# Crossed 64x64 and 32-row tiles for a convolution kernel's MLP, and fp32 band products from whole-sample row sums without rounded parts

## The reference, cut to what matters

```python
x = x + conv3x3_mixed(_gn(x))      # L0: weights mixed from 3 experts by a softmax of pooled features
x = x + depthwise3x3(abs(_gn(x)))  # L1
x = x + box17x17(_gn(x))           # L2: mean over 17x17, zero padding
x = x + mlp(neighbour_sum(_gn(x))) # L3
```

```python
xn = jnp.repeat(nbr, 8, axis=1)
h = elu(w1 @ xn); h = elu(w2 @ h); h = elu(w3 @ h); h = elu(w4 @ h)
F_int = w5 @ h                     # then mean over groups of four, times 0.1
```

## Time and profile before

| what | value |
| --- | --- |
| median of 3 runs | 909.75 us (906.79 to 911.74) |
| profiled execution, its own time | 903.43 us |
| its span | 901.6 us |
| mean granted TensorE clock | 0.92 of full speed |
| DMA moved | 64.70 MB, mean 72 GB/s |

### The profile page before, as it was taken

The page is one execution under the profiler, slowest core; times in us unless marked ns, Lnnn a source line. Parts: engine busy times, 40 slices in busy tenths (PEclk is TensorE's granted clock), DMA queues, the critical chain, the costliest instruction groups (busy, mean ns, idle before and its releaser), DMA issues.

```text
span 901.6 us, 11198 instructions
## 1 busy us (share of the span) xinstructions
PE 706.5 (78%) x3313; PEld 317.0 (35%) x3313; DVE 676.7 (75%) x1166; ACT 593.4 (66%) x1105; POOL 267.2 (30%) x310
## 2 busy tenths in 40 slices
PE   1424556848897989888888889798989888989993
PEld 0211223224342435343434434353525343434330
DVE  1442744848879887988888878978797789858994
ACT  0120121639777888679876978688977788888883
POOL 2010236212721163223622181116311632271110
PEclk9976678869999999999999999899999999989997
DMA  6528491435512360215320541136022302002201
GB/s 112 119 68 164 83 194 41 88 58 111 113 30 53 78 148 18 64 44 122 74 64 3 120 100 44 37 82 141 19 65 65 65 19 64 19 17 46 54 19 47
DMA packets 54421, 64.70 MB, mean 72 GB/s; under 512 B 6626, under 2 KB 39922, under 8 KB 54386
## 3 DMA queue, kind: packets, MB, share of 16 engines
q1 hardware_dynamic: 52256, 62.98, 32.5%
q10 hardware_dynamic: 2130, 1.30, 0.8%
HBM read 9.34 MB, written 8.39 MB: 20 GB/s over the span
## 4 chain that ended last, share of the span: by engine, by line
PE 38%; DVE 21%; ACT 17%; DMA 7%; issue 6%; POOL 5%; SPq 3%; ACTq 1%; DVEq 0%; POOLq 0%
PE pz L721 18%; PE pc L661 8%; PE pc L702 7%; ACT u L595 6%; ACT u L603 6%; DMA xs<-in_x_dram 4%; DVE g L909 4%; DVE bn L830 3%; DVE box_sum L946 3%; DVE u L905 3%; ACT u L600 2%; PE pz L717 2%; POOL box_sum L479 2%; POOL box_sum L477 2%; DMA win<-y 2%
## 5 line engine op out<-in xcount | busy, mean ns | idle before, releaser
L721 PE MATMUL pz<-g,wT 128*128 128x512 f32 x768 | 366.9, 617 | 15.4 <-DVE g L909 14.8
L909 DVE SCALAR_TENSOR_TENSOR g<-u,pz 128x512 f32<-128x512 f32 x476 | 310.9, 682 | 88.2 <-ACT u L603 83.9
L595 ACT ACTIVATE u<-pz 128x512 f32<-128x512 f32 x472 | 276.6, 597 | 136.2 <-PE pz L721 109.6
L603 ACT ACTIVATE u<-u 128x512 f32<-128x512 f32 x472 | 287.4, 637 | 1.3
L721 PEld LDWEIGHTS pz<-g,wT 128*128 128x128 f32 x768 | 142.2, 195 | 215.5 <-DVE g L909 110.0
L702 PE MATMUL pc<-win,t 64*32 64x512 f32 x1536 | 114.9, 734 | 67.7 <-DMA win<-y 32.0
L830 DVE BATCH_NORM_STATS2 bn<-xs 128x6 f32 (+1 forms) x128 | 87.1, 688 | 27.1 <-DMA xs<-in_x_dram 16.9
L717 PE MATMUL pz<-stack,w1T 128*128 128x512 f32 x256 | 83.1, 447 | 24.0 <-DMA stack<-near_rest 15.8
L460 POOL TENSOR_TENSOR stat<-stat,con 128x1 f32<-128x1 f32 x32 | 17.9, 560 | 276.2 <-DVE stat L850 276.2
L702 PEld LDWEIGHTS pc<-win,t 64*32 64x32 f32 x1536 | 32.9, 123 | 139.8 <-issue 139.7
L468 POOL TENSOR_TENSOR box_part<-box_sum,box_part 128x512 fp32r<-128x512 f32 x32 | 38.7, 1211 | 142.9 <-ACT box_part L577 142.9
(11 more groups left out here) (91 smaller groups left out, 569.2 us busy)
## 6 DMA issues: line engine op xcount, KB each, us to landing
win<-y SPq DMA_DIRECT2D x62, 260.0 KB, 4.5
win<-y SPq DMA_DIRECT2D x62, 195.0 KB, 4.5
xs<-in_x_dram SPq DMA_DIRECT2D x8, 1024.0 KB
stack<-near_rest SPq DMA_DIRECT2D x64, 128.0 KB, 2.3
out_dram<-xs SPq DMA_DIRECT2D x8, 1024.0 KB
stack<-stack SPq DMA_DIRECT2D x32, 128.0 KB, 2.2
win<-y SPq DMA_DIRECT2D x31, 65.0 KB, 4.6
win<-y SPq DMA_DIRECT2D x31, 56.9 KB, 4.4
```

What stands on the lines that cost most here:

```text
L595: act.activation(u[:, m, :], pz[:, m, :], ACT.Relu, scale=-1.0, bias=0.0).then_inc(relu_done, 1)
L603: act.activation(u[:, m, :], u[:, m, :], ACT.Exp, scale=-1.0).then_inc(exp_done, 1)
L721: pe.matmul(pz[:, m, :], wT[:, l - 1, :], g[:, m, :], start=True, stop=True).then_inc(z_mm, 1)
L909: dve.scalar_tensor_tensor(out=elus(j, q, l)[:, m, :], in0=u[:, m, :], scalar=-1.0, in1=pz[:, m, :], op0=ALU.add, op1=ALU.max).then_inc(g_ ...
```

## The change

The band products of box and neighbour sums take unrounded fp32 sums of a whole sample (with a row of zeros at either end); rounding, subtraction and their four semaphores go. The MLP takes `near` itself: layer 0 uses 32 rows per tile m, one fp32 product each. Layers 1 to 3 use two 64x64 products for each m, on the diagonal quarters of the array for even m and on the other two for odd m, so that an odd tile's halves change places at each of these layers; `w5T` has a version for either order. The POOL splits and the SP moves go, and the sync queue keeps the stores, windows and loads. `wnat` and its transposes shrink from 7 to 4 tables.

```diff
-        box_sum = sb("box_sum", [P, 2, KB * PITCH])
-        box_part = [sb(f"box_part{n}", [P, K + 2, W], F32R) for n in range(2)]
-        near_sum = box_sum[:, :, :].rearrange(...)
-        near_part = [sb(f"near_part{n}", [P, K + 2, W], F32R) for n in range(2)]
-        box_mat = sb("box_mat", [P, 3, P], F32R)
-        near_mat = sb("near_mat", [P, 3, P], F32R)
+        box_sum = sb("box_sum", [P, K + 2, PITCH])
+        near_sum = sb("near_sum", [P, K + 2, W])
+        box_mat = sb("box_mat", [P, 3, P])
+        near_mat = sb("near_mat", [P, 3, P])
...
-        near_rest = sb("near_rest", [P, CH], F32R)
-        stack = [sb(f"stack{n}", [P, CH], F32R) for n in range(2)]
...
-        w1T = [sb(f"w1T{n}", [P, M, P], F32R) for n in range(2)]
-        wT = sb("wT", [P, 3, P])
-        w5T = sb("w5T", [P, 32])
+        wT = sb("wT", [P, 4, P])
+        w5T = sb("w5T", [P, 2, 32])
...
 # SP
-                if mlp:
-                    stack_rests(t - 1, 1)
-                    if not (isinstance(t, int) and t == 1):
-                        store(t - 2)
-                    stack_rests(t - 1, 2)
+                if mlp and not (isinstance(t, int) and t == 1):
+                    store(t - 2)
                 if early:
                     windows1(t + 1)
-                if mlp:
-                    stack_rests(t - 1, 3)
                 if more:
                     windows0(sp, t + 2, range(2))
-                if late:
-                    stack_rests(t, 0)
...
 # POOL
             def near_sums(i, c):
                 if c == 0:
                     pool.wait_ge(y3_written, i + 1)
-                if c >= 2:
-                    pool.wait_ge(near_low, Q * i + c - 1)
-                y = blocks(y3, c)
+                    if not (isinstance(i, int) and i == 0):
+                        pool.wait_ge(conv_mm[3], Q * i)
+                y, o = blocks(y3, c), own_rows(near_sum, c)
...
             def one(t, early, late, mlp, more):
-                if mlp:
-                    split_near(t - 1, 1)
-                if late:
-                    lower_box(t, 0)
-                    lower_box(t, 1)
-                    lower_box(t, 2)
                 if more:
                     scales(t + 2, 0)
                 if early:
                     scales(t + 1, 1)
                 if late:
-                    lower_box(t, 3)
-                if mlp:
-                    split_near(t - 1, 2)
-                if late:
                     scales(t, 3)
-                if mlp:
-                    split_near(t - 1, 3)
-                if late:
-                    near_sums(t, 0)
-                    near_sums(t, 1)
-                    lower_near(t, 0)
...
+                    for c in range(Q):
+                        near_sums(t, c)
...
-                if late:
-                    split_near(t, 0)
 # ACT
-                        if p == 0 and l > 0 and late:
-                            round_box(t, l - 1)
-                        if p == 1 and l == 0 and late:
-                            round_box(t, 3)
...
-                        if p == 2 and l >= 2 and late:
-                            round_near(t, 2 * l - 4)
-                            round_near(t, 2 * l - 3)
 # PE
-            def banded(o, mats, parts, j):
+            def banded(o, mats, rows, j):
                 for d in range(3):
-                    for n in range(2):
-                        last = pe.matmul(o, mats[:, d, :], parts[n][:, j * KB + d:(j + 1) * KB + d, :],
-                                         start=d == 0 and n == 0, stop=d == 2 and n == 1)
+                    last = pe.matmul(o, mats[:, d, :], rows[:, j * KB + d:(j + 1) * KB + d, :], start=d == 0, stop=d == 2)
...
-                    pe.wait_ge(box_low, Q * i + min(j + 2, Q))
+                    pe.wait_ge(box_rows, Q * i + min(j + 2, Q))
...
             def layer(j, q, l):
+                top, bottom = slice(0, HID), slice(HID, P)
                 for m in range(M):
                     if l == 0:
...
                         if m == 0:
-                            pe.wait_ge(stack_in, STACK * (Q * j + q + 1))
-                        for n in range(2):
-                            last = pe.matmul(pz[:, m, :], w1T[n][:, m, :], stack[m // 2][:, :], start=n == 0, stop=n == 1)
-                        last.then_inc(z_mm, 1)
+                            pe.wait_ge(conv_evac[3], Q * j + q + 1)
+                        pe.nop(nofuse=True)
+                        rows = slice(32 * m, 32 * m + 32)
+                        pe.matmul(pz[:, m, :], wT[rows, 0, :], near[rows, q * CH:(q + 1) * CH],
+                                  start=True, stop=True).then_inc(z_mm, 1)
                     else:
                         pe.wait_ge(g_written, zn(j, q, l - 1, m))
-                        pe.matmul(pz[:, m, :], wT[:, l - 1, :], g[:, m, :],
-                                  start=True, stop=True).then_inc(z_mm, 1)
+                        pe.nop(nofuse=True)
+                        for rows, to in ((top, bottom), (bottom, top)) if m % 2 else ((top, top), (bottom, bottom)):
+                            last = pe.matmul(pz[to, m, :], wT[rows, l, rows], g[rows, m, :], start=True, stop=True)
+                        last.then_inc(z_mm, 1)
...
-                    last = pe.matmul(po[32 * m:32 * m + 32, :], w5T[:, :], elus(j, q, LAYERS - 1)[:, m, :],
+                    last = pe.matmul(po[32 * m:32 * m + 32, :], w5T[:, m % 2, :], elus(j, q, LAYERS - 1)[:, m, :],
...
 # DVE, box_scan
-                if c >= 2:
-                    dve.wait_ge(box_low, Q * i + c - 1)
+                    if not (isinstance(i, int) and i == 0):
+                        dve.wait_ge(conv_mm[2], Q * i)
                 n = KB * PITCH
-                dve.tensor_tensor_scan(box_sum[:, c % 2, :], y2[:, c * n + BOX:(c + 1) * n + BOX],
+                dve.tensor_tensor_scan(own_rows(box_sum, c).rearrange("p k w -> p (k w)"), y2[:, c * n + BOX:(c + 1) * n + BOX],
```

More of the change, by code:

```diff
@@ L450, in _ @@
             pool.memset(y2[:, :], 0.0).then_inc(zeroed, 1)
[L451 to L454 removed]
+            for t in (box_sum, near_sum):
+                pool.memset(t[:, 0, :], 0.0).then_inc(zeroed, 1)
+                pool.memset(t[:, K + 1, :], 0.0).then_inc(zeroed, 1)
+            pool.wait_ge(zeroed, 11)
             pool.wait_ge(s_early, 16)
@@ L765, in _ @@
             pe.wait_ge(setup_dve, 2)
-            for n in range(M + 3):
+            for n in range(4):
                 last = pe.transpose(pz[:, :, :].rearrange("p a n -> p (a n)")[:, n * P:(n + 1) * P], wnat[:, n, :], const("ident"))
@@ L783, in setup_natural @@
                 dve.wait_ge(setup_dve, 1)
-                for m in range(M):
-                    for p in range(2):
-                        for at in range(p * C + m % 2 * 2 * C, P, HID):
-                            last = dve.tensor_copy(wnat[p * HID:(p + 1) * HID, m, at:at + C], w1eff[p * HID:(p + 1) * HID, :])
+                for p in range(2):
+                    for at in range(p * C, P, 2 * C):
+                        last = dve.tensor_copy(wnat[p * HID:(p + 1) * HID, 0, at:at + C], w1eff[p * HID:(p + 1) * HID, :])
                 last.then_inc(setup_dve, 1)
```

88 lines of the change are left out of this document (16 added, 72 removed).

## The result

The kernel after the change takes 877.61 us (median of four runs, 876.75 to 880.01) against 910.03 for the kernel before (four runs): a ratio of 0.965, 95% interval 0.962 to 0.969. The point forecast was 887, with 860 to 905 around it. The profiled execution took 878.26 (span 876.2) where that of before took 903.43 (span 901.6), so its own difference is 25.2 us against a predicted 23. A run over 1.5% above the fastest of its kernel counts as slow and is left out of every ratio and interval: one run each of warm, late_full, after_again and act_loads; medians are over all runs.

What follows compares the result with a forecast made beforehand. No engine is full; the prediction saw a round as a relay between engines. Round 1 (−9.0 and −2.2), five middle rounds (−8.5) and round 7 (−3.1) sum to −23, taking 909.75 to 887 us, range 860 to 905.

Steps and rivals of the forecast that it cites:

- group sums to the relu of layer 1, quarter 1: Middle round: the longer chunk falls partly into the 1.2 GHz stretch, 6.0 us where it was 3.75, so +2.2.
- Tiles of the MLP: Layers 1 to 3: a pair of 64x64 products takes 0.91 us, two pairs 1.0, against 0.86 for one 128x128 product.
- Band chunks: Six one-pass products (1.39 us) become three fp32 ones, 2.67 with the change of tile form: +1.28 for each of 64 chunks.
- the loop: Quarters 1 and 3: two layers chained through last join, last product, chunk and next product take 9.9 us, 4.95 a layer.
- the chunk isn't paid for: Rival: neighbouring products don't run side by side, PE needs 6.1 us a layer with a chunk, 949 us in all; chance 0.07.
- Rounding and POOL's subtractions: They go, with waits in ACT's queue and long DVE scans beside POOL; gain between 0 and 2.0 us, 1.7 taken.
- quarter 0's −1.7: Quarter 0 of a middle round gets 1.7 us shorter, from two of four scans being long, as DVE rarely waits there.
- Round 1: Without SP moves behind input loads, quarter 1's group sums come at 186.4, relu −9.0 us; rest of the round −2.2.
- round 7: −3.1: Round 7: −3.8 from roundings gone, less chunk and pace; quarter 1 chunk +1.3, pace +0.4, scan −1.0; sum −3.1 us.
- round 8: 0: Round 8: no change, since DVE and ACT operations are untouched and the tiles' products hide beside them.
- The rival of the clock: PE idles more; a chunk at 1.2 GHz costs 2.57 us more, with half of 56 such chunks 959 us; chance 0.05.
- One bank, one row tile: Rival: both halves of a product queue, 1.72 us each, a layer 6.9, about 1,110 us in all; chance 0.02.

Runs made afterwards that it cites:

- warm: The kernel after with extra 128x128 products, results unread, filling TensorE's waits ahead of layer 0, group sums and some late layers: 884.2 us.
- late_full: The kernel after with one 128x128 product per tile in layers 1 to 3 of round 7 (quarters 0 and 2) and round 8: 885.0 us.
- after_again: The kernel after, unchanged, measured again beside the kernels with a 128-row layer 0: 882.3 us, or 879.9 without its one run of 895.2.
- act_loads: The kernel before with the input loads of samples 5 to 7 moved from SP's queue to ACT's: 908.6 us, ratio 0.997.
- uncrossed: The kernel after with all 64x64 products on the diagonal of the array, odd tiles no longer using the other two quarters: 931.4 us.
- bands_only: The kernel before with only the new bands (three fp32 products of unrounded sums), MLP, splits and SP moves as before: 1.6% slower, +13.8 us.
- full_tiles: The kernel after with one 128x128 product per tile in layers 1 to 3 in place of two 64x64 ones: 919.3 us.
- padded_late: The kernel after with layer 0 of rounds 7 and 8 as one 128x128 product per tile, weights zero outside the 32 rows: 874.2 us.
- padded: The kernel after with layer 0 as one zero-padded 128x128 product per tile in every round: five runs, 873.2 to 877.5 us.
- split_chunk: The kernel after with each band chunk's first product set between tiles 1 and 2 of layers 1 to 3, the other two after: 898.2 us.

## Why the prediction was right, and where it was not

The sign and the total hold, and so do most steps of a middle round; the near agreement of the total rests on the two misses that cancel. One middle round (round 3), by the prediction's own steps:

```
step                                             before   after   change  predicted
quarter 0 (relu of layer 0 to the group sums)     31.67   28.10    -3.57    -1.7
group sums to the relu of layer 1, quarter 1       3.75    5.58    +1.83    +2.2
to the relu of layer 2, quarter 2                 28.42   27.13    -1.29    -1.3
to the group sums of quarter 3                    15.23   12.60    -2.63    -2.6
to the relu of layer 1 (the longer chunk)          2.79    4.12    +1.33    +1.3
three layer intervals of quarter 3                14.06   14.67    +0.61    +0.4
sum                                               95.92   92.20    -3.72    -1.7
```

- **Tiles of the MLP: right.** 0.49 a tile (two crossed pairs in 1.0), and uncrossed shows that this needs the crossing. On the rule of the Trainium skill (TensorEngine Tiling (Array Packing), Gotcha 1: PSUM Pressure), by which row tiles can't use one bank at a time, the trace again disagrees: both row halves write the tile's one bank, and 1.95 us for eight products leaves no room for eight turns of 0.86, nor for four.
- **Band chunks: right in quarter 3** (2.77 to 2.84 against 2.67, the loop 9.98 against 9.9). The rival "the chunk isn't paid for" is what bands_only, full_tiles and uncrossed show: 6.01 us for a layer and its chunk in bands_only, where it had 6.1, and 919 to 931 us. The crossed tiles hold it off.
- **Rounding and POOL's subtractions: the mis-sized term is quarter 0's −1.7.** I had reasoned from two long scans and added that DVE rarely waits there. Measured is −3.57. The second conv pair shows where it is: it waited 2.37 us for DVE's evacuation and, behind that wait, ran 1.6 us longer at low clock (4.42 against 2.81). A delay on DVE was paid twice, once as a wait and once as PE's clock. The same pair took 4.2 to 4.5 us in each of rounds 1 to 5; ahead of the mark of round 6 it waited 1.54 and took 2.81 (664.14), and there quarter 0 gains only 0.6 more than forecast. Together that is about 8 of the 12.5 us by which the middle beat the forecast. Some 3 more are low stretches that the kernel before has and round 3 has not: a layer from 535.42 to 540.14 in quarter 3 of round 4, 1.7 us longer than its like (the clock is 0.76 from 533 to 540 us), and a first box chunk wholly at 1.2 GHz in round 5 (584.41, 2.91 us), 1.2 us. The forecast, made from round 3, couldn't have them.
- **Round 1: right in kind.** Group sums at 183.54 against a predicted 186.4, and the relu behind them at 189.27 against 192.4. Of the 2.9 us more, some 1.9 would be quarter 0 again (its second conv pair took 4.34 before and 2.81 after). act_loads bears out that the queue's order held quarter 1's move back, since its product comes 5.6 us earlier there, and adds that reordering alone gives no gain.
- **Round 7 and round 8: wrong.** The steps "round 7: −3.1" and "round 8: 0" failed. The prediction said that layer 0's small products hide beside round 8's work, and costed them by their duration alone. In time they do hide. What came with them is PE's lower clock at three places: 8.6 us between the tails of the kernel after and of padded_late. The other 4 us of the miss are read from padded_late's tail, where the clock stays up in rounds 7 and 8. 2.2 are quarters 1 and 2 of round 6, where its first conv pair (673.20) waits 2.60 us and then takes 4.40 at the lower clock, against 0.99 and 2.81 in the kernel before. From the group sums of quarter 3 in round 6 to the first chunk of round 7 it grew by 1.9, quarter 1 of round 7 by 2.3 and its quarter 3 by 2.2, where I had 1.7, 0.7 (with a scan's −1.0 in it) and 1.7. Quarter 2 of round 7 gained 4.7 for a predicted 5.5, and round 8 gained 1.2 for a predicted 0. Part of the 4.7 is the low stretch at 799.28, which the kernel before has and the prediction did not see in its row of 10.5 us.
- **The rival of the clock** was counted too narrowly. I priced chunks at 1.2 GHz and looked for idle time as the cause. Idle time is not enough for the low places of the tail: with the same 1.9 us of it in the 8 us ahead, the clock fell behind 32-row products and did not behind 128-row ones.
- **A sum of a rival is off.** The terms of *One bank, one row tile* add up to 1,142 and not to 1,110 us. It changes nothing, as the measured layer rules that rival out.

## What to carry to other kernels

Split a product into quarter-array tiles only where a crossed neighbour runs beside it: uncrossed pairs cost as much as whole products. Two edits that bound each other should be priced together, since here one alone is slower, the other 2.8% faster and both 3.5%. When a small-row product is paced by another engine, look at the granted clock behind it and try the same product padded with zero rows. Filling an idle gap that ends at a fixed wait gained nothing here. And compare the parts of a kernel with the terms of a forecast even where the total agrees.

## What the runs showed of the hardware

- **32-row products and the clock.** Layer 0's four 32x128 products, one for each join, were followed by the 1.2 GHz level at three places where 128x128 products with the same numbers (zeros in the other 96 rows) kept 2.4 GHz: 0.72 against 1.00 in eight microseconds with PE equally busy in them and ahead of them. It isn't so each time: over the traces the level fell at 29 of 40 such places with 32 rows and at 2 of 25 with 128, and in quarter 1 of a middle round it falls with 128 rows too, behind 1.71 us of idle time (5.37 us for padded's layer 0). Beside this the Trainium skill (TensorE: Matmul & The Clock Gate, "Why this matters for your kernels") says that a product of 32 rows takes as long as one of 128, and that the gain is in running several at a time. The trace agrees where inputs wait (all four in 1.14 us at 155.27 us of the kernel after, four in a row of 0.86 being 3.4). Where joins set the pace, one a microsecond, little can run side by side: 3.86 us at 827.32. Why the clock falls more often with fewer rows stays open.
- **Four 64x64 fp32 products at a time**, on all four quarters of the array: 1.95 us for eight (1.88 from start to start), about half of the 3.58 us for the same eight uncrossed.
- **Changing between 128x128 and 64x64 products** costs about 0.25 us a time by split_chunk, an estimate (5.17 against 4.65 us for two more changes).
- **The same kernel varies**: four runs of the kernel after in one session lay within 3.3 us, six of the same kernel in another within 21 (874.4 to 895.2), and in the trace of after_again single rounds are 1 to 2 us longer (94.24 from the mark of round 2 to that of round 3, against 92.27).
